# Second attention turned round: scores in two orientations, maxima subtracted by PE, V and ones stationary

## The reference

```
q, k, v = split(norm(x) @ W_qkv + b)           # 256 tokens, 16 heads of 8
q, k    = rope(q), rope(k)
p       = softmax(q @ k.T / sqrt(8))            # 256 x 256
out     = concat over heads(p @ v) @ wo + bo
x       = x + out
```

## Time and profile before

| | us |
|---|---|
| median of 3 runs | 548.98 (541.31 to 555.68) |
| the profiled execution | 544.12 |
| its span | 542.3 |
| PE busy | 416.3 (77%) |
| DVE busy | 404.0 (74%) |
| ACT busy | 307.4 (57%) |
| POOL busy | 128.4 (24%) |

### The profile page before, as it was taken

How to read it: one execution, slowest core, us unless ns; L and a number is a source line. 1 busy time by engine, 2 the same in 40 slices (tenths; PEclk the granted TensorE clock), 3 DMA queues, 4 the chain that set the end, 5 groups by cost and what they waited for, 6 DMA issues and landing times.

```text
span 542.3 us, 8231 instructions
## 1 busy us (share of the span) xinstructions
PE 416.3 (77%) x2672; PEld 311.0 (57%) x2673; DVE 404.0 (74%) x1032; ACT 307.4 (57%) x969; POOL 128.4 (24%) x125
## 2 busy tenths in 40 slices
PE   4899999999988799666998999799992531055564
PEld 4656576576565486356897899688452421013353
DVE  4379679879799652976996888876259559979794
ACT  1564665864755424469789788555631861275252
POOL 1000000000000056400085854300663013272101
PEclk9999999999999979888999899999798555555597
DMA  8940000000000000000000000000000000000001
GB/s 311 445 152 2 1 0 2 1 1 1 2 0 1 1 2 0 0 1 0 2 2 1 2 2 0 2 1 2 0 1 1 0 0 2 0 0 1 1 0 39
DMA packets 3841, 13.32 MB, mean 25 GB/s; under 512 B 372, under 2 KB 2420, under 8 KB 3284
## 3 DMA queue, kind: packets, MB, share of 16 engines
q1 hardware_dynamic: 3800, 12.80, 6.0%
HBM read 12.28 MB, written 0.52 MB: 24 GB/s over the span
## 4 chain that ended last, share of the span: by engine, by line
PE 49%; DVE 28%; ACT 12%; issue 7%; POOL 2%; DMA 1%; POOLq 0%; SPq 0%; ACTq 0%; DVEq 0%
PE bank L887 6%; PE bank L864 5%; ACT big L480 4%; PE bank L907 4%; PE bank L935 4%; PE bank L921 4%; DVE area L1296 3%; ACT tab_ L480 3%; PE bank L949 3%; PE bank L892 3%; DVE area L1299 2%; DVE nmax L1440 2%; DVE tab_ L1296 2%; PE bank L1006 2%; PE bank L850 2%
## 5 line engine op out<-in xcount | busy, mean ns | idle before, releaser
L480 ACT ACTIVATE big<-bank,nmax 128x256 f32<-128x256 f32 x128 | 59.2, 473 | 29.7 <-DVE nmax L1474 16.3
L480 ACT ACTIVATE tab_<-bank,nmax 128x256 f32<-128x256 f32 x128 | 59.3, 467 | 26.9 <-DVE nmax L1440 24.8
L864 PE MATMUL bank<-vpad,xT 128*128 128x96 f32 x512 | 69.5, 280 | 5.0 <-DVE xT L1446 4.7
L864 PEld LDWEIGHTS bank<-vpad,xT 128*128 128x128 f32 x512 | 63.7, 195 | 9.1 <-DVE xT L1446 8.1
L480 ACT ACTIVATE area<-bank 128x512 f32<-128x512 f32 (+3 forms) x68 | 36.9, 550 | 53.0 <-PE bank L892 16.2
L1440 DVE TENSOR_REDUCE nmax<-bank 128x2 f32<-128x512 f32 x64 | 43.5, 679 | 10.3 <-PE bank L841 10.0
L1482 DVE COPY area<-bank 128x512 f32<-128x512 f32 x64 | 42.3, 683 | 10.2 <-PE bank L921 10.2
L396 POOL TENSOR_TENSOR rstd<-rstd,halves 128x2 f32<-128x2 f32 x4 | 2.8, 699 | 182.0 <-DVE rstd L1299 182.0
L1446 DVE COPY xT<-bank 128x512 f32<-128x512 f32 x64 | 43.4, 677 | 1.8 <-PE bank L850 1.5
L921 PE MATMUL bank<-tabs,big 128*128 128x128 f32 x256 | 37.6, 278 | 7.8 <-DVE big L1299 7.8
L921 PEld LDWEIGHTS bank<-tabs,big 128*128 128x128 f32 x256 | 29.8, 141 | 23.6 <-DVE big L1299 14.2
(11 more groups left out here) (219 smaller groups left out, 888.9 us busy)
## 6 DMA issues: line engine op xcount, KB each, us to landing
w2s<-w SPq DMA_DIRECT2D x1, 4352.0 KB, 26.7
rows<-row SPq DMA_DIRECT2D x1, 1600.0 KB, 11.3
w0s<-w SPq DMA_DIRECT2D x3, 512.0 KB, 7.2
w1s<-w SPq DMA_DIRECT2D x1, 1408.0 KB, 16.2
w0s<-w SPq DMA_DIRECT2D x1, 1024.0 KB, 13.3
xs<-x SPq DMA_DIRECT2D x1, 512.0 KB, 4.6
out<-tab_ SPq DMA_DIRECT2D x2, 256.0 KB, 2.3
tabs<-tab SPq DMA_DIRECT2D x1, 421.5 KB, 5.7
```

Source lines behind the costliest of these rows:

```text
L480: return nc.scalar.activation(o, i, f, **kw)
L864: m = mm(bank[4 + gslot][:, o:o + v(k).shape[1]], A.pT[:, half, k, q * P:(q + 1) * P], v(k), start=(k == 0), stop=(k == QT - 1))
```

## The change

The attention loop of layer 1 is rewritten.

- Each head's scores are computed twice. `scores1` is as before and serves only the maximum. `scores_less_max`, 14 steps later (`LAG`), computes them with keys by rows: kaM stationary, queries moving, 256 columns, for two key tiles. In the same accumulation it adds the negated maxima: a second product with `msel`, one column of a 0/1 table repeated 128 times with stride 0, as the stationary, and `mT`, the turned maxima of eight heads (high and low parts), moving.
- The maxima of eight heads are split (`max_parts`, DVE), turned (`turn_max`, PE) and copied (`take_max`, ACT).
- One exponent over 128 x 512 for each head (`exponents1`), without bias or row sum. Its output is already turned, so there are no transposes and no DVE copy.
- `values1`, every four heads: V of a head (8 columns and a column of ones, 32 columns read) is stationary, the probabilities move, 256 columns; the four heads go to four groups of 32 output partitions of bank 4. The ones column gives the row sums. ACT copies the result (`take_values`), PE turns it at the end of a batch (`turn_values`), DVE divides (`normalise1`).
- Only batch 0 is projected, rotated and turned before the loop. The other batches' projection, rotation, splitting and turning stand in fixed steps of the loop (`QKV_STEP` and the following), one batch ahead. They share banks 5 and 6 in a written order.
- All key tiles are filled by ACT: four before the loop, up to head 15 four steps ahead, from head 16 on one step ahead, at the end of the step.
- The loop has 86 steps where it had 68; the conditioning's steps are moved, its products use bank 7 alone, and its scratch rows lie elsewhere.
- POOL fills the V tile with ones in place of a small strip of zeros. DVE copies `msel` before the first projection is taken, and PE waits for that copy before the first projection.

```diff
+        LAG = 14
+        STEPS = NH + 22
+        MAX_PARTS, MAX_TURN, MAX_TAKE = 8, 9, 10
+        VALUES, VALUES_TAKE, OUT_TURN, OUT_TAKE = LAG + 5, LAG + 6, LAG + 19, LAG + 20
+        ATT_TURN, ATT_TAKE, ATT_OUT, ATT_ADD = 52, 53, 54, 56
+        QKV_STEP, ROPE_STEP, HIGH_STEP, LOW_STEP, PART_STEP = (1, 3), (2, 4), (7, 8), (8, 9), (9, 10, 13, 14)
...
 ACT
+            def mask_key(n):
+                if n < 4:
+                    act.wait_ge(S("kaM_zero"), 1)
+                if n >= H:
+                    act.wait_ge(S("a1_ST"), n - H + 1)
+                act.wait_ge(S("a1_taken"), 4 * (n // H) + 4)
+                dst, src = masked_key(n)
+                acti(dst, src, ACT.Copy).then_inc(S("a1_kM"), 1)
...
+            def exponents1(n):
+                act.wait_ge(S("a1_ST"), n + 1)
+                if n >= 6:
+                    act.wait_ge(S("a1_PV"), (n - 6) // 4 + 1)
+                acti(pT1[n % 6], bank[2 + n % 2][:, :], ACT.Exp).then_inc(S("a1_exp"), 1)
...
-            for n in range(NH):
-                if n == OUT_STEP + 2:
+            for i in range(4):
+                mask_key(i)
+            for i in range(STEPS):
+                for o in octet(i, MAX_TAKE):
+                    take_max(o)
+                if 0 <= i - LAG < NH:
+                    exponents1(i - LAG)
+                if i + 4 < H:
+                    mask_key(i + 4)
+                for g in quad(i, VALUES_TAKE):
+                    take_values(g)
+                for m in of_batch(i, HIGH_STEP):
+                    high_parts(m)
+                for n in of_batch(i - 1, PART_STEP):
+                    take_part(n)
+                if H <= i + 1 < NH:
+                    mask_key(i + 1)
+                if i == ATT_TAKE:
                     take_outputs(0)
-                core_exp(A1, n, n % 3, n % 2, (n // 4) % 2, n % 4, n // 4 if n % 4 == 0 else None)
-                if n + H < NH:
-                    dst, src = masked_key(n + H)
-                    acti(dst, src, ACT.Copy).then_inc(S("a1_kM"), 1)
-                weave(n)
+                weave(i)
...
 PE
+            def scores1(n):
+                g, at = n % H // 4, n // H % 2 * SEQ
+                pe.wait_ge(S("a1_kM"), n + 1)
+                if n < 2:
+                    pe.wait_ge(S("x_ready"), 2)
+                else:
+                    pe.wait_ge(S("a1_max"), n - 1)
+                for q in range(QT):
+                    m = mm(bank[n % 2][:, q * SEQ:(q + 1) * SEQ], qaT[:, g, at + q * P:at + (q + 1) * P],
+                           kaM[:, n % H, :], start=True, stop=True)
+                m.then_inc(S("a1_S"), 1)
...
+            def scores_less_max(n):
+                g, at = n % H // 4, n // H % 2 * SEQ
+                pe.wait_ge(S("a1_mTs"), n // 8 + 1)
+                if n >= 2:
+                    pe.wait_ge(S("a1_exp"), n - 1)
+                for k in range(QT):
+                    to = bank[2 + n % 2][:, k * SEQ:(k + 1) * SEQ]
+                    mm(to, kaM[:, n % H, k * P:(k + 1) * P], qaT[:, g, at:at + SEQ], start=True, stop=False)
+                    m = mm(to, msel[:, n % 8:n % 8 + 1].to_broadcast([P, P]), mT[:, n // 8 % 2, :],
+                           start=False, stop=True)
+                m.then_inc(S("a1_ST"), 1)
+
+            def values1(g):
+                pe.wait_ge(S("a1_exp"), 4 * g + 4)
+                if g >= 1:
+                    pe.wait_ge(S("a1_o"), g)
+                for k in range(QT):
+                    for n in range(4 * g, 4 * g + 4):
+                        at = n % H * (DH1 + 1)
+                        m = mm(bank[4][head_rows(n), 0:SEQ], vz[:, n // H * QT + k, at:at + 32],
+                               pT1[n % 6][:, k * SEQ:(k + 1) * SEQ], start=(k == 0), stop=(k == QT - 1))
+                m.then_inc(S("a1_PV"), 1)
...
-            for i in range(NH + 3):
+            for i in range(STEPS):
+                for o in octet(i, MAX_TURN):
+                    turn_max(o)
                 if i < NH:
...
+                    scores1(i)
+                if 0 <= i - LAG < NH:
+                    scores_less_max(i - LAG)
+                for t in of_batch(i, QKV_STEP):
+                    qkv1(t)
+                for n in of_batch(i, PART_STEP):
+                    turn_part(n)
+                for g in quad(i, VALUES):
+                    values1(g)
+                for n in out_tile(i, OUT_TURN):
+                    turn_values(n)
...
 DVE
+            for i in range(STEPS):
+                for o in octet(i, MAX_PARTS):
+                    max_parts(o)
+                if i < NH:
+                    top1(i)
+                for t in of_batch(i - 1, QKV_STEP):
+                    take_qkv(t)
+                for t in of_batch(i - 1, ROPE_STEP):
+                    rope(t)
+                for m in of_batch(i, LOW_STEP):
+                    low_parts(m)
+                for n in out_tile(i, OUT_TAKE):
+                    normalise1(n)
```

More of the change, by code:

```diff
@@ L499, in squares @@
                 m.then_inc(S("squared"), 1)
[L501 to L507, removed]
-                    e = acti(A.prob[:, slot, q, :], bank[half][:, q * SEQ:(q + 1) * SEQ], ACT.Exp,
-                             bias=nmax[:, half, q:q + 1], accum_out=rsum[:, gslot, q, hg:hg + 1])
-                e.then_inc(S(A.tag + "_exp"), 1)
             act.wait_ge(S("mod0"), 1)
@@ new lines, in mask_key, with take_part @@
+            def mask_key(n):
[6 more added lines that the diff above has]
+                acti(dst, src, ACT.Copy).then_inc(S("a1_kM"), 1)
+            def take_part(n):
+                act.wait_ge(S("a1_part"), n + 1)
+                if n >= 8:
+                    act.wait_ge(S("a1_kM" if n % 4 < 2 else "a1_ST"), H * (n // 4 - 1))
+                acti(part_place(n), bank[shared_bank("part", n)][:, :].rearrange("p (g t) -> p g t", g=2), ACT.Copy
+                     ).then_inc(S("a1_taken"), 1)
@@ L1039, in _, with to_shared, qkv1 @@
[L1039 to L1045 removed]
+            def to_shared(kind, n):
+                sem, count = shared_taken(kind, n)
+                pe.wait_ge(S(sem), count)
+                return bank[shared_bank(kind, n)]
+            def qkv1(t):
+                pe.wait_ge(S("xT"), 2 * NB + t // QT + 1)
+                to = to_shared("qkv", t)
+                mm(to[:, 0:3 * P], xT[:, t * P:(t + 1) * P], part(w1s, W1, "qkv"), start=True, stop=True
+                   ).then_inc(S("a1_qkvmm"), 1)
@@ new lines, in turn_values @@
+            def turn_values(n):
+                b, q = n // QT, n % QT
+                pe.wait_ge(S("a1_o"), 4 * b + 4)
+                to = to_shared("out", n)
+                for g in range(4):
+                    m = nc.tensor.transpose(to[:, g * P:(g + 1) * P], oT[:, g, q * P:(q + 1) * P], ident)
+                m.then_inc(S("a1_oT"), 1)
+            pe.wait_ge(S("msel"), 1)
+            for t in range(QT):
+                qkv1(t)
+            normed_T("n1a", 1)
+            for n in range(4):
+                turn_part(n)
@@ L1632, in row_factors @@
+            dve.wait_ge(S("vz_ones"), 1)
+            V.tensor_copy(msel[:, :], part(tabs, TAB, "msel")).then_inc(S("msel"), 1)
+            for t in range(QT):
+                take_qkv(t)
+                rope(t)
+            rms_norm("n1a", 1)
+            for m in range(2):
+                low_parts(m)
             def row_factors(name):
@@ L1928, in shape_tables @@
     t[:, slice(*at["blocks"])] = (p[:, None] // DH1 == p[None, :] // DH1)
+    msel = np.zeros((P, 8), np.float32)
+    for h in range(8):
+        msel[2 * h:2 * h + 2, h] = 1.0
+    t[:, slice(*at["msel"])] = msel
     t[:, slice(*at["inv_n"])] = np.array([1.0 / size for _, size in QUANT], np.float32)
```

364 lines of the change are left out of this document (171 added, 193 removed).

## The result

The changed kernel takes 579.6 us (median of 4 runs, 575.39 to 584.12), where the kernel before, beside it on the same chip, took 552.33: 1.062 times as long [1.053, 1.071]. It is slower. (Some runs of either kernel are longer as a whole at a lower granted clock; the ratio leaves them out, which is why it isn't 579.6/552.33 = 1.049.) The profiled execution took 575.39 us with a span of 573.6 us, against the 544.12 and 542.3 of before. So 31.3 us of span have to be found.

A forecast was written before the change was run, and what follows sets the result against it. The prediction took a ring of waits between TensorE and ScalarE, 1.96 us a trip over 48 steps, as the bound. Its steps summed to turn_outputs(1) at 376.4, 0.2 less than before; plus 2 for clock: 546 profiled, 551 median, range 526 to 582.

The forecast's parts named there:

- the link from exponent to mask: ScalarE's exponent over 128x512 in each trip: the mask starts 0.49 us after it, at worst 0.57.
- the ring: Steps 15 to 62: scores, less-max scores, exponent, mask, next scores wait in a loop, 1.96 us a trip; chance 0.50.
- the cover of TensorE's other work: In the ring: value products (0.9), projections (0.64) and turns (0.44) fit in 1.2 us free, costing nothing.
- Step 1: Before the heads: two tiles projected and rotated first, first scores at 234.5 against 247.2, 12.7 us gained.
- Steps 3 and 4: Loop steps 15 to 62: 48 trips at 1.96 us, 94.1, plus 11.8 for ScalarE's work between exponent and mask.
- Step 5: Loop steps 63 to 78, without masks: TensorE sets them, 13.9 us, then the last head drains, until 376.4.
- the allowance for the clock: 2 us added for some trips at a low clock, as TensorE has thin work in steps 0 to 14.
- the engines' own work sets the pace: Rival for loop steps 15 to 62: 1.4 us a trip, 27 us less, 524; faster or unbound ring: chance 0.20.
- TensorE's link: In the ring, from score records to the waiting engine, with four more records at 0.12: 1.02 us, at most 1.18.
- The bursts: ScalarE work between exponent and mask: take_values 3.3 us, high parts and part copies 6.5, Silu 2.0, together 11.8.
- The rival "the clock": Full clock not held in the ring: TensorE's 0.75 us doubles in 48 steps, +35, 586 us; chance 0.07.
- The value products: Four heads' products overlap, 0.9 us, at no cost in the ring; rival, one behind the other: 588, chance 0.05.

The follow-up runs named there:

- experiment 1: Changed kernel with mask_key issued ahead of the exponent in each step, except at a layer part's first head: 538.85 us, 0.989 of the kernel before.
- experiment 5: Changed kernel with LAG 11 in place of 14, order of each step kept: 570.93 us, 1.054 of the kernel before.
- experiment 7: Changed kernel plus a second, unread mask copy in 45 steps, between exponent and mask: 1.103 of the kernel before.
- experiment 8: Changed kernel plus the same 45 unread mask copies, issued ahead of the step's exponent: 1.073 of the kernel before.
- experiment 2: Changed kernel with the mask still behind the exponent, but ahead of take_values, high parts and part copies: 1.046 of the kernel before.
- experiment 9: Changed kernel with LAG 11, masks two steps ahead, and msel copied earlier, in VectorE's pause behind mlp_out(0): 529.4 us, 0.975 of the kernel before.
- experiment 10: As experiment 9, plus 11 unread products of weights on TensorE ahead of the turns of parts: 526.56 us, 0.971 of the kernel before.
- experiment 3: Changed kernel plus five unread TensorE products at the end of about half of the ring's steps: 1.059 of the kernel before.

## Why the prediction was wrong

It forecast 551 us and no difference; the kernel is 6.2% slower by the ratio. To a slower kernel it gave a chance of 0.30, and the time lies at the edge of its range. The mechanism was right, its price was not: the link from exponent to mask, the clock in the ring, the cover of TensorE's other work and the steps behind the last scores were priced too low. Against the forecast of 546 for the profiled execution, 29.4 us are missing. They lie in these steps of its sum:

| step of the sum | forecast | measured | missing |
|---|---|---|---|
| 1, first scores | 234.5 | 238.6 | 4.1 |
| 2, steps 0 to 14 | 18.1 | 19.2 | 1.1 |
| 3 and 4, steps 15 to 62 | 105.9 | 123.6 | 17.7 |
| 5, step 63 to turn_outputs(1) | 17.9 | 24.5 | 6.6 |
| 6, behind it, against before | 0 | 2.0 | 2.0 |
| the allowance for the clock | 2 | in the rows above | -2 |

- **The ring, right.** Its four links are as described, the waits are put down to the two lines that the prediction named, and experiments 1, 5, 7 and 8 show that it, and not the engines' work or the release of the tile, sets the pace. The rival "the engines' own work sets the pace" is out; even with the ring cut a step costs 1.76 us, not the 1.4 of that rival. One slip in the working: bounds of 1.91 and 2.05 us a trip are 549 to 555 us, not 541 to 561; the bare trip came out at 2.09, above 2.05 and below the wider bound of 2.2.
- **TensorE's link, right:** 1.02 forecast, 1.02 measured. The pitch of 0.12 holds at full clock for both kinds of product, and the stationary that is read with stride 0 costs nothing extra.
- **From exponent to mask, mis-sized: the first failed term.** I took 0.49, from two activations in a row that both read a bank. It is 0.62 in nearly every trip: the mask starts only when the exponent has ended. With 0.46 in place of 0.45 for the mask and the start behind it, a trip is 2.09 to 2.10: 48 x 0.13 = 6.2 of the 17.7 us. Where the mask did start 0.49 behind the exponent, in step 51, the trip took 1.95 us, as forecast:

```profile
354.57 0.60 ACT L532 ACTIVATE big<-bank 128x512 f32<-128x512 f32 x1 [0.46 <-PE bank L1127]
355.06 0.40 ACT L532 ACTIVATE kaM<-kaT 32x256 fp32r<-32x256 f32 x1
```

  In the same trace a copy that reads a bank starts 0.49 after an exponent:

```profile
280.21 0.60 ACT L532 ACTIVATE tab_<-bank 128x512 f32<-128x512 f32 x1 [0.59 <-PE bank L1127]
280.70 0.38 ACT L532 ACTIVATE area<-bank 128x256 f32<-128x256 f32 x1
```

  It would be easy to say that the mask is later because it reads SBUF (kaT), but that isn't it. In experiment 8 a mask, with the same source, starts 0.49 behind too:

```profile
269.47 0.60 ACT L533 ACTIVATE tab_<-bank 128x512 f32<-128x512 f32 x1 [0.62 <-PE bank L1134]
269.96 0.40 ACT L533 ACTIVATE kaM<-kaT 32x256 fp32r<-32x256 f32 x1
```

  There all five masks that follow an exponent directly and go to rows 0 to 31 of kaM did so, and all 21 that go to other rows took 0.62. In the changed kernel the 21 in other rows took 0.62 as well, but so did four of the five in rows 0 to 31. So the rows have to do with it, and what else does stays open.
- **The bursts, right.** take_values +0.28 a trip, parts +0.5, as forecast; the Silu step took 4.67 us, 2.1 over a trip with its part copy, where 2.0 was priced. Experiment 2 took most of the first two back.
- **The clock, mis-sized: the second failed term, and the larger one.** Steps 3 and 4 at their measured bare trip and bursts come to 48 x 2.09 + 11.8 = 112.1 us; 11.5 us are left, where 2 were allowed. About 9 of them are trips at the low clock, where a bare trip takes 2.77 in place of 2.09. The prediction held that a ring with TensorE busy 2.6 of 4 us keeps the clock, because windows of 4 us with 2.24 and 1.63 busy had it at 1.00. Over the 48 steps it was 0.86. But that busy share alone doesn't decide it: with 65% it stood at 1.00 from 337.5 to 371 us of the same trace, and with 69% in the 60 us of experiment 2. The stretches as a whole had 0.96 with the ring cut (experiment 1), 0.94 with the bursts moved, 0.86 in the changed kernel and 0.67 with the extra copy in the ring, so more waiting went with a lower clock; experiment 8 (0.80 at the same bare trip) doesn't fit in, and what starts a low stretch stays open. The rival "the clock" was right in kind, and priced at its extreme (35 us).
- **The cover of TensorE's own work, held to be complete: a third failed term, smaller.** The prediction put the projections, value products and turns at nothing, as they have 1.2 us in each trip. Steps 19 and 35 have a projection and value products and took 2.56 us at full clock, 0.47 over the bare trip. The two steps with turn_values are long too: step 34 was 0.73 over at full clock, and step 33, partly at the low clock here, was 0.90 over at full clock in experiment 8. Together about 2.6 of the 11.5 us.
- **Step 5, mis-sized:** I let TensorE set the steps after the last scores, at 0.48 each for the less-max products. There is a second, smaller loop there. With two banks, scores_less_max(n) waits for the exponent of n-2, and the exponents come 0.75 apart at best (397.17, 397.92, 398.65, 399.42), so 15 of them cost 4 us more than priced. The other 2.6 of the 6.6 us aren't taken apart; in the first 3.5 us of these steps the clock stood at 0.50. The drain behind the last exponent was 4.05 us, where 4.0 was priced.
- **Step 1, mis-sized in part by the clock:** the msel wait cost its 0.9 us (experiment 9), and layer 0 ended 0.9 us later in this execution. Of the other 3.2 us, experiment 10, with a higher clock in this stretch, got 1.5 back; the clock stood at 0.50 here from 224 to 238 us, and how much of the rest is its doing isn't shown. The 1.1 us of step 2 and the 2.0 of step 6 aren't taken apart.
- **The value products, right.** By the rule of the Trainium skill that the prediction weighed (TensorE: Matmul & The Clock Gate, Part 3, The mechanism), a weight load overlaps a matmul in flight only when its row group differs. The prediction worked out from it that the four products would run one behind the other. The trace contradicts it for four column groups as for two: 16 records in 1.07 us, where 16 behind one another would take 3.4 at the 0.215 of the earlier trace rows.

## What to carry to other kernels

Before you count what a change takes off the engines, walk once around every loop of the waits: if an engine's next input is made behind an operation that waits for that engine in the same step, the loop's latency is the period, and idle engines don't help. Such a loop is cut by moving one instruction ahead in its queue (39 us here), not by less work. And don't price a latency-bound loop at full clock because single windows with the same busy share had it. In the versions of this ring the clock was between 0.67 and 0.94, and each trip at the low clock took 2.77 us in place of 2.09; what moves the clock was not settled here.

## What the runs showed of the hardware

- On ScalarE the next operation started either 0.49 us or 0.62 us behind a 0.60 us exponent. A 128-row copy from a bank had 0.49, a mask of rows among 32 to 127 had 0.62 (all 21 in the changed kernel and in experiment 8), a mask of rows 0 to 31 had either. Two copies of 0.41 us on the same 32 rows started 0.32 apart (experiment 7), masks of neighbouring heads, on other rows, 0.42 to 0.44 (the changed kernel, heads 0 to 11).
- F32R records of 256 columns have a pitch of 0.12 us at full clock, also in a chain that alternates between two stationaries, one of them a column read with stride 0.
- With products added that nobody reads, the granted clock was higher: 0.87 against 0.74 in 224 to 238 us (experiment 10 against 9), 1.00 against 0.83 in 302 to 342 us (experiment 3). These are single executions, and experiment 2 had 0.96 in the second stretch without any.
- The copy of 128x8 to msel took 0.79 us where it stood, with a GpSimd operation beside it, and 0.17 us in its new place in experiment 9, with none beside it. What made it long wasn't tried.
